# Gathers of the first expert layer on GpSimd: a wait for the last but one before each, and the last sixteen by pairs of tiles

## The reference, cut to what matters

```python
logits = jnp.einsum('bsh,eh->bse', x, router_w) + expert_bias
scores = jax.nn.softmax(logits, axis=-1)
top_w, top_idx = jax.lax.top_k(scores, TOP_K)            # TOP_K = 4 of 16
top_w = top_w / jnp.sum(top_w, axis=-1, keepdims=True)
g = jnp.einsum('bsh,khe->bske', x, gate_proj)            # 256 -> 224
u = jnp.einsum('bsh,khe->bske', x, up_proj)
out = jnp.einsum('bske,keh->bskh', silu(g) * u, down_proj)
sel = jnp.take_along_axis(out, top_idx[..., None], axis=2)
return jnp.sum(sel * top_w[..., None], axis=2)
...
x = _layernorm(x + _L0_ffn_ref(x, ...), axis=-1)
```

## Time and profile before

| | |
|---|---|
| median of 3 runs | 645.86 us (643.99 to 651.1) |
| the profiled execution | 640.31 us |
| its span, first to last instruction | 638.5 us |
| mean granted TensorE clock | 0.917 |
| busy: PE, PEld, DVE, ACT, POOL | 85%, 69%, 50%, 35%, 55% |

### The profile page before, as it was taken

One profiled execution on the slowest core, in us unless ns is written; L12 is line 12 of the kernel. 1 busy time (PEld: TensorE's weight loads), 2 busy tenths in 40 slices (PEclk: granted clock), 3 DMA queues, 4 the chain that ended last, 5 costly groups with the idle time before them and its releaser, 6 DMA issues.

```text
span 638.5 us, 9610 instructions
## 1 busy us (share of the span) xinstructions
PE 543.3 (85%) x3085; PEld 443.2 (69%) x3085; DVE 322.4 (50%) x718; ACT 223.6 (35%) x526; POOL 349.1 (55%) x316
## 2 busy tenths in 40 slices
PE   8899876047999996729898977799999999999995
PEld 4666665036998885718664534788888888888885
DVE  4655785513566442303469895754343433334365
ACT  4655442113555663312351201254222222222233
POOL 3474115676578985460017885105575585769190
PEclk9989996577999996868898986989999999999998
DMA  8999881244667665441000005200532523423111
GB/s 261 376 384 385 303 275 67 83 140 121 197 196 226 199 203 164 118 113 34 0 1 1 1 0 149 74 2 10 145 104 68 153 75 100 124 86 120 53 66 67
DMA packets 72865, 83.71 MB, mean 131 GB/s; under 512 B 7617, under 2 KB 63698, under 8 KB 72818
## 3 DMA queue, kind: packets, MB, share of 16 engines
q1 hardware_dynamic: 33490, 38.90, 20.0%
q10 hardware_dynamic: 35968, 35.26, 16.6%
q0 software_dynamic: 3360, 8.93, 4.4%
HBM read 48.61 MB, written 34.47 MB: 130 GB/s over the span
## 4 chain that ended last, share of the span: by engine, by line
PE 65%; DVE 10%; issue 9%; DMA 4%; ACT 2%; POOL 1%; ACTq 0%; another core or an unknown queue 0%; DVEq 0%
PE PS L1839 47%; DMA FA<-xg 4%; PE PS L2063 2%; DVE FA L1797 2%; DVE PS L1779 2%; PE PS L2181 2%; PE PS L2292 1%; PE PS L2205 1%; PE PS L1936 1%; PE PS L1914 1%; PE PS L2106 1%; PE PS L2076 1%; POOL xg L691 1%; PE PS L2304 1%; PE PS L2060 1%
## 5 line engine op out<-in xcount | busy, mean ns | idle before, releaser
L1839 PE MATMUL PS<-XH,EW 128*128 128x512 f32 x400 | 132.0, 395 | 0.0
L1839 PE MATMUL PS<-EW,XH 128*128 (+2 forms) x252 | 80.1, 402 | 9.8 <-issue 8.5
L1839 PEld LDWEIGHTS PS<-XH,EW 128*128 128x128 f32 x400 | 75.2, 188 | 16.3 <-DVE EW L1200 0.5
L1569 DVE TENSOR_TENSOR FA<-OGATE,PS 128x512 f32<-128x512 f32 x42 | 28.9, 688 | 107.8 <-ACT OGATE L1008 92.4
L1839 PE MATMUL PS<-XL,EW 128*128 128x512 f32 x200 | 78.6, 393 | 0.0
L1008 ACT ACTIVATE OGATE<-PS 128x512 f32<-128x512 f32 x48 | 28.7, 599 | 126.8 <-PE PS L1839 126.8
L801 POOL TENSOR_TENSOR FA<-FA,QT 128x1024 f32<-128x1024 f32 (+1 forms) x16 | 37.4, 2338 | 59.6 <-DVE FA L1797 59.6
L1839 PE MATMUL PS<-EW 128*128 128x256 f32 x288 | 63.1, 284 | 0.5 <-DVE W1L L1574 0.4
L1839 PEld LDWEIGHTS PS<-EW,XH 128*128 128x128 f32 x252 | 46.6, 206 | 15.9 <-issue 10.3
L1839 PE MATMUL PS<-EW,W1L 128*128 128x256 f32 x192 | 54.3, 283 | 0.0
L1839 PEld LDWEIGHTS PS<-EW 128*128 128x128 f32 x288 | 49.1, 189 | 3.9 <-DVE W1L L1574 1.2
(11 more groups left out here) (385 smaller groups left out, 1232.0 us busy)
## 6 DMA issues: line engine op xcount, KB each, us to landing
xg<-EQ ACTq DMA_DIRECT2D x1, 16384.0 KB, 60.4
EG<-in_gateup SPq DMA_DIRECT2D x16, 448.0 KB, 4.0
yg<-EQ ACTq DMA_DIRECT2D x1, 6016.0 KB, 20.3
FA<-xg ACTq DMA_DIRECT2D x47, 128.0 KB
yg<-FA ACTq DMA_DIRECT2D x47, 128.0 KB, 2.1
ED<-in_down SPq DMA_DIRECT2D x16, 224.0 KB, 4.9
EG<-in_gateup SPq DMA_DIRECT2D x16, 192.0 KB
FA<-in_gateup SPq DMA_DIRECT2D x16, 192.0 KB, 3.0
```

Source lines behind the costliest of these rows:

```text
L1569: dve.tensor_tensor(mixed[:, i % MIXED, :], sil_t[:, i % 2, :], bank(step_bank(i) + 1), ALU.mult).then_inc(mixed_dve, 1)
L1839: ins = pe.matmul(o, l, r, start=start and i == 0, stop=stop and i == n - 1, skip_group_check=True)
```

## The change

`gather` gets a wait ahead of its DMA. A list `asked` holds the gathers in the order in which they are issued, over all three batches; from the third on, each waits until the one that was issued two before it has landed. The sixteen of the last batch change their order: before, both choices of tile 0, both of tile 1, and so on; now, for each pair of tiles, choice 2 of both, then choice 3 of both. In that order two successive gathers never count on the same semaphore. The number of gathers, their data, and everything on the other engines are as before.

```diff
+            asked = []
+
             def gather(t, k):
 
+                if len(asked) >= 2:
+                    before, pick = asked[-2]
+                    pool.wait_ge(back_ld[before], 16 * (pick + 1))
+                asked.append((t, k))
                 n = t * TOP0 + k
                 pool.indirect_dma_start(
                     out=BACK[t][:, k, :], out_offset=None, in_=yg,
...
                 for t in range(NT):
                     gather(t, k)
             stored_up_to(TOP0 - 1, 2)
-            for t in range(NT):
+            for p in range(NT // 2):
                 for k in range(2, TOP0):
-                    gather(t, k)
+                    for t in (2 * p, 2 * p + 1):
+                        gather(t, k)
             pool.wait_ge(tiles_done, SLOT_TILES)
```

## The result

| | before | changed |
|---|---|---|
| median | 646.31 us (643.99 to 651.1, 4 runs) | 630.02 us (627.46 to 632.86, 4 runs) |
| the profiled execution, its span | 640.31, 638.5 us | 629.74, 627.9 us |
| mean granted TensorE clock | 0.917 | 0.924 |

The ratio is 0.974, with an interval of 0.970 to 0.979: the change is faster, by 16.3 us between the medians and 10.6 us between the two profiled executions (that of before was 6.0 us quicker than its median, and the traces don't show what the other runs had more). The forecast was 648. In all tables a median is over all runs of a kernel, and a ratio leaves out the runs that lie over 1.5% above its fastest one.

A forecast was written before the change was run, and what follows sets the result against it. TensorE, with 65% of the chain, was taken as the bound, 26.0 us being lost to its late signals beside gathers. Added disturbance of 2.5 us, order nothing: 640.31 became 642.8, median 645.86 became 648.4, stated as 648; range 632 to 659.

The forecast's parts named there:

- If TensorE loses time at the same rate while gathers run: Slot tiles beside gathers: 0.66 us lost per us of gathers, so 4.1 us more cost 2.7 us; 2.5 taken.
- Just two are in flight in the second and third batches already: Gather batches: at 2.48 us to land and 1.26 between starts; argued against the faster rival.
- The batches' growth: Three gather batches at a pace of 1.39 us: longer by 1.0, 1.0 and 2.1 us, together 4.1.
- the upper bound of 2.15 for the first batch: Gather pace in us from a load's 4.0 us landing under traffic plus 0.3; the first batch would grow by 7.1.
- There are 19 us of cover: Pair sums: last gather lands about 289.3, the last pair's first product with tile 7 starts at 308.82.
- a rival's term: Faster rival's limit at the pair sums: third batch starts at some 258, last pair's sum ends near 285, not 310.7.
- TensorE's signals get through sooner: Slot tiles beside gathers: fewer DMAs in flight free the signals; half of 26.0 us gives median 633; chance 0.26.
- full release to 621: Faster rival with all lost time out of reach: gathers limit the pair sums, 25 us gained, 621 us.
- The order of the last sixteen: Third gather batch: pairs complete after as many gathers as before, so the new order gives nothing in either direction.
- The gathers become long, and TensorE is held until the last has landed: Third batch, slower rival: later last landing delays the kernel us for us; 654 or 667 us; chance 0.24.

The follow-up runs named there:

- b0_before: The kernel before, unedited, traced in a session without late signals: 603.41 us, ratio 1.002.
- e1: The kernel before with only the new order of the last sixteen gathers, no added waits: 644.34 us, ratio 1.000.
- e4: Changed kernel with landing waits replaced by one tiny waited-for GpSimd instruction before each gather but the first: 628.86 us, ratio 0.976 to before.
- e3: Changed kernel with each gather waiting for the one just before it, one in flight: 672.59 us, ratio 1.043 to before.
- e2: Changed kernel with three gathers allowed in flight, last sixteen ordered by fours of tiles: 640.83 us, ratio 0.993 to before.
- e15: The kernel of e10 run again in a session with late signals: 635.38 us, ratio 0.993 to before.
- e16: The kernel of e15 plus a tiny waited-for GpSimd instruction before each of sixteen scatters: 627.81 us, ratio 0.982 to before.
- e5: Changed kernel with landing waits replaced by two tiny waited-for instructions before each gather but the first; no late signals: 616.61 us, ratio 1.020 to before.
- L2: Later session with late signals, running e15 and e16 beside the kernel before, which took 640.01 us.
- e10: Changed kernel without landing waits; one tiny waited-for instruction before gathers of the first two batches only, except the first: 603.20 us, ratio 0.998 to before.
- T2: Later session with signals on time, running b0_before, e10 and others; the kernel before took 603.02 us.
- T3: Later session with signals on time, running the kernel of e10, the changed kernel and others; the kernel before took 600.98 us.
- T1: Later session with signals on time, running the changed kernel, e5 and others; the kernel before took 603.05 us.

## Why the prediction was wrong

- **"If TensorE loses time at the same rate while gathers run"**, from which +2.5 us followed, is the step that failed. The loss over the last ten SiLU steps fell from 26.0 to 27.5 - 23.7 = 3.8 us while the gathers took longer, and b0_before has 3.0 of that 3.8 without any late signals. The denser the gathers are issued, the larger it is: 56.2 us of ten steps at 1.26 (e1), 35.5 at 1.46 (e4), 27.5 at two in flight, 25.7 at one (e3).
- **"Just two are in flight in the second and third batches already"** was the argument that gave this step its chance. Landing was put at 2.48 us, after the scatter; it is 2.77 in the third batch and 4.5 in the first. At 1.26 us between starts that is over two, and three to four, an estimate, since both landings were measured with the waits in place. The waits held in all three batches. The Trainium skill, "DMA: Bandwidth & Descriptors", section "Anatomy of one DMA — SWDGE (gpsimd) path", by which the estimate was 2.3 us, is further off still; the measured 2.77 and 4.5 decide.
- **The batches' growth** was mis-sized with it: forecast 1.0, 1.0 and 2.1 us, measured 5.2, 3.9 and 4.7 (14.1, 12.7 and 23.6 us from first to last start, against 8.9, 8.8 and 18.9 in the earlier trace rows). The pace came out at 1.57 where 1.39 was taken; the upper bound of 2.15 for the first batch was near its 2.02.
- **"There are 19 us of cover"** was true of that trace, and was made of the late signals, as the prediction itself had said it might be. They went, and the gathers became the limit: a rival's term had this, with the last pair's sum ending near 285. It ended near 297, by the pace of 1.57 and a batch that began at 267.8 and not 258.
- **The rival "TensorE's signals get through sooner"** named the mechanism and, at half, 633 us. It had 0.26. What spoke for it (the loss stands only beside gathers, and they pile up beyond two in the first batch) should have weighed more than an argument from 0.3 us of landing time. Its full release to 621 was not reached, for the reason above.
- **The order of the last sixteen is worth nothing**: right (e1, 1.000).
- **"The gathers become long, and TensorE is held until the last has landed"**: not in the changed kernel. e2, e15 and e16, with an unbroken last batch at 1.26 us, do start the pair sums 3 to 6 us behind the last gather's start; a longer batch with gaps (the change, e4) releases TensorE in between.
- Not foreseen at all: that the late signals would be absent in three of six sessions. Where they are absent, the sum is simple and of the other sign: nothing to win at the signals, and 10 to 13 us lost at the pair sums; 1.018, 1.019 and 1.018.

Open stays whether pace or number in flight governs. The waits lower both (mean pace 2.02, about 1.8 and 1.57 us), e4 sets the first alone and is two thirds of the cure at 1.46, and e15's ratio fell to the side of the number in flight, for a reason that its last batch explains but no run tested. e5's 1.73 under late signals would tell, and was not run in L2. Waits with the old order were not tried, since two successive gathers then count on one semaphore. What makes the signals late in a session, and by what path GpSimd's DMAs hold TensorE's signals, no run shows. No version was found that is ahead in both kinds: e10's kernel is even with before in T2 (0.998), 0.6% behind in T3 and 0.7% ahead in L2; the change is 2.6% ahead in the first session and 1.8% behind in T1 to T3.

## What to carry to other kernels

Where a consumer starts many us behind the matmul it waits for, and only beside one kind of work, try that work at another density before you cost the edit by its own duration: a disturbance need not go by time. A throttle on transfers pays once and costs once; look up what will wait for their end when the disturbance is gone, since the cover seen in the old trace may be made of it. And measure the kernel before again with every comparison: a gain that removes a disturbance is a loss wherever the disturbance is absent.

## What the runs showed of the hardware that was not expected

- In three of six sessions TensorE's signals reach ScalarE up to 11.6 us late while GpSimd issues gathers 1.26 us apart, and late too beside scatters 1.28 us apart; VectorE was 4.0 us late in e4. One tiny instruction between them takes two thirds of it away beside the gathers (a pace of 1.46 us; 56.2 to 35.5 us, a floor of 23.7) and most of it beside the scatters (1.50 us; 34.9 to 25.0 us, 23.1 without the effect).
- The same kernel took 646, 645 and 640 us in three sessions and 603, 603 and 601 in three others, the lowest single run of the first three (636.4) above the highest of the others (613.2); the difference lies in those two stretches.
- An indirect DMA of 128 rows of 1 KB landed after 2.77 us in a stretch with a DMA share of 0.30, and after 4.5 us in one with 0.70 (one gather each).
- The granted clock was 1.00 in the third batch of b0_before, where TensorE was busy for 19.70 of 19.80 us, and 0.77 in that of the earlier trace rows, where it was busy for 8.41 of 19.80.
